# Score products on one half of the array's rows each, and experts selected by maximum and replacement

## What is computed

```python
def reference(x, w_q, b_q, w_k, b_k, w_v, b_v, w_o, b_o, gate_w, e_bias, up_w, down_w, shared_up_w, shared_down_w):
    h = layernorm(x)
    q, k, v = (heads(h @ w.T + b) for w, b in ((w_q, b_q), (w_k, b_k), (w_v, b_v)))
    attn = softmax(einsum('bhtd,bhsd->bhts', q, k) / sqrt(8))
    x = x + layernorm(einsum('bhts,bhsd->bhtd', attn, v) @ w_o.T + b_o)
    h = layernorm(x)
    scores = sigmoid(h @ gate_w.T)                      # [token, 32]
    sc = scores + e_bias
    group_scores = top_k(sc.reshape(T, 8, 4), 2)[0].sum(-1)
    kept = the 4 groups with the largest group_scores   # top_k: of equal ones the first
    idx = top_k(where(kept, sc, 0), 6)[1]
    w = scores[idx] / (scores[idx].sum(-1) + 1e-20) * 2.5
    f = sum over idx of w * relu(h @ up_w[e].T)**2 @ down_w[e].T + relu(h @ shared_up_w.T)**2 @ shared_down_w.T
    return x + layernorm(f)
```

## Time and profile before

| | |
|---|---|
| time, median of 3 runs | 581.74 us (580.57 to 582.0) |
| profiled execution: its own time | 586.01 us |
| span of that execution, first to last instruction | 584.0 us |
| PE busy | 539.0 us (92%) |
| PEld busy | 317.0 us (54%) |
| DVE busy | 422.9 us (72%) |
| ACT busy | 434.9 us (74%) |
| POOL busy | 148.2 us (25%) |
| mean granted TensorE clock | 0.962 |

### The profile page before, as it was taken

How to read it: one execution, slowest core, us unless ns; L and a number is a source line. 1 busy time by engine, 2 the same in 40 slices (tenths; PEclk the granted TensorE clock), 3 DMA queues, 4 the chain that set the end, 5 groups by cost and what they waited for, 6 DMA issues and landing times.

```text
span 584.0 us, 10389 instructions
## 1 busy us (share of the span) xinstructions
PE 539.0 (92%) x3248; PEld 317.0 (54%) x3248; DVE 422.9 (72%) x1116; ACT 434.9 (74%) x879; POOL 148.2 (25%) x439
## 2 busy tenths in 40 slices
PE   2478998999999999999989999999999999999993
PEld 1224554556655556555546665656566565656551
DVE  6676685788888778778857968686885868576343
ACT  2326676788888878776788787979888797977773
POOL 6141121213243223221102114224042423202010
PEclk9559798999999999999999999999999999999997
DMA  6333374233333333323000000000000000000001
GB/s 176 105 113 89 106 237 122 86 103 102 103 103 93 108 111 94 93 91 97 18 3 1 1 1 1 19 1 1 20 0 20 0 20 1 17 2 1 19 0 36
DMA packets 42774, 33.75 MB, mean 58 GB/s; under 512 B 4032, under 2 KB 35392, under 8 KB 42464
## 3 DMA queue, kind: packets, MB, share of 16 engines
q1 hardware_dynamic: 42720, 33.09, 18.6%
HBM read 18.01 MB, written 14.68 MB: 56 GB/s over the span
## 4 chain that ended last, share of the span: by engine, by line
PE 72%; DMA 8%; SPq 8%; ACT 5%; DVE 4%; issue 2%; POOL 0%; ACTq 0%; DVEq 0%
PE pY L1184 11%; PE pS L1184 11%; PE pO L1101 7%; PE pS L1089 6%; PE pS L1161 6%; PE pS L1163 6%; PE pS L1078 6%; PE pS L1162 6%; PE pS L1170 5%; DMA k_scratch<-k_parts 4%; DMA kp<-k_scratch 4%; SPq L369 3%; SPq L357 3%; ACT probs L557 3%; SPq L377 1%
## 5 line engine op out<-in xcount | busy, mean ns | idle before, releaser
L771 DVE TENSOR_REDUCE mneg<-pS 128x2 f32<-128x512 f32 x256 | 164.2, 686 | 37.6 <-PE pS L1078 36.2
L557 ACT ACTIVATE probs<-pS 128x512 f32<-128x512 f32 x256 | 140.9, 599 | 47.5 <-PE pS L1089 46.5
L947 DVE TENSOR_TENSOR h_ring<-pS,rr 128x512 f32<-128x512 f32 x128 | 88.3, 690 | 75.6 <-ACT rr L634 73.4
L625 ACT ACTIVATE r<-pS 128x512 f32<-128x512 f32 x144 | 85.7, 595 | 42.4 <-PE pS L1163 37.7
L1078 PE MATMUL pS<-kp,qp 96*128 96x256 bf16 x512 | 103.2, 287 | 12.3 <-DMA kp<-k_scratch 11.6
L1089 PE MATMUL pS<-qp,kp 102*128 102x512 bf16 x256 | 99.7, 392 | 4.5 <-ACT probs L557 2.8
L634 ACT ACTIVATE rr<-r 128x512 f32<-128x512 f32 x128 | 80.9, 632 | 4.0
L1161 PE MATMUL pS<-qp,up_hi 128*128 128x512 f32 x144 | 82.7, 574 | 0.1
L1078 PEld LDWEIGHTS pS<-kp,qp 96*128 96x128 bf16 x512 | 45.3, 101 | 58.7 <-DMA kp<-k_scratch 15.7
L1184 PE MATMUL pS<-h_ring,down_sb 128*128 128x512 f32 x144 | 73.5, 592 | 0.0
L1184 PE MATMUL pY<-h_ring,down_sb 128*128 128x512 f32 x144 | 73.0, 592 | 0.0
(11 more groups left out here) (182 smaller groups left out, 758.1 us busy)
## 6 DMA issues: line engine op xcount, KB each, us to landing
qp<-q_scratch SPq DMA_DIRECT2D x64, 96.0 KB
kp<-k_scratch SPq DMA_DIRECT2D x64, 96.0 KB
q_scratch<-q_parts SPq DMA_DIRECT2D x16, 192.0 KB, 2.0
k_scratch<-k_parts SPq DMA_DIRECT2D x16, 192.0 KB, 2.1
q_scratch<-q_parts SPq DMA_DIRECT2D x16, 128.0 KB, 1.9
k_scratch<-k_parts SPq DMA_DIRECT2D x16, 128.0 KB, 2.0
out_x<-ot SPq DMA_DIRECT2D x7, 256.0 KB, 2.3
q_scratch<-q_parts SPq DMA_DIRECT2D x16, 64.0 KB, 1.7
```

What stands on the lines that cost most here:

```text
L557: nc.scalar.activation(probs[j][:, sh], pS2[n % S2_RING][:, :, :], ACT.Exp, scale=SCALE).then_inc(exp_done, 1)
L625: nc.scalar.activation(r_sb[k % 2][:, :], pU[k % 2], ACT.Relu).then_inc(relu_done, 1)
L771: nc.vector.tensor_reduce(mneg[u % 2][:, :, hh, k], pS1[n % S1_RING][:, :].rearrange("p (a s) -> p a s", a=TH), AX.X, ALU.max, negate=True ...
L947: nc.vector.tensor_tensor(h_sb[n % HRING], pC[k % 2], r2_sb[k % 2][:, :], ALU.mult).then_inc(h_done, 1)
```

## The change

Scores: head `hh` = 0 now stands in rows 0 to 50 (48 and 3 for the maximum) and `hh` = 1 in rows 64 to 114. A product takes one head's rows alone, so 48 or 51 rows in one half of the array, and `qp` needs no zeros. The key product is now made per head, 2 x 128 keys by 256 queries, instead of for two heads at once. In `scores_by_both` the products alternate: queries' of one head, keys' of the other, and again, each time in the other half of the rows. Both waits (for `max_done` and `exp_done`, at a unit's first step also `packed` and `m_packed`) stand ahead of the four. `probs` is laid out by head first. The preset zeros of `qp` go away; the ones of `kp` now lie at two places of each slot. `x_cut`, `x_hi`, `x_lo` of the experts' part get other places.

Experts: MAX8 gives the largest 8, `match_replace` replaces the 4 (6) largest by a marker, first occurrence first, and a comparison with the marker gives the selection. 23 waits in 8 steps.

```diff
-DIFF_ROWS = 2 * QK_ROWS + 2 * M_ROWS
+DIFF_ROWS = QK_ROWS + M_ROWS
+HALF = P // 2
+KEY_HEADS = (1, 0)
-ROUTE_AT = ((3, 4, 5, 6, 7, 8, 9, 10, 11, 12, 13, 14),
-            (0, 1, 2, 3, 4, 5, 6, 8, 9, 11, 12, 13))
+ROUTE_AT = ((3, 4, 5, 6, 7, 8, 9, 11),
+            (0, 1, 2, 3, 4, 5, 6, 8))
...
-               ((5, 6), (7,), (), (8, 9), (10, 11), (), (), ()))
+               ((), (5,), (), (6,), (7,), (), (), ()))
...
-                    rows = slice(QK_ROWS * hh, QK_ROWS * (hh + 1))
-                    for dst, scratch in ((qp[u % RING][rows, hh], q_scratch), (kp[u % RING][rows], k_scratch)):
+                    rows = slice(HALF * hh, HALF * hh + QK_ROWS)
+                    for dst, scratch in ((qp[u % RING][rows], q_scratch), (kp[u % RING][rows], k_scratch)):
...
             write_parts(0)
-            sp.wait_ge(preset, 1)
             sp.wait_ge(ones_set, 1)
...
-            for i in range(RING):
-                ins = nc.gpsimd.memset(qp[i][:, :, :, :].rearrange("p a b c -> p (a b c)").bitcast(F32), 0.0)
-            ins.then_inc(preset, 1)
...
-                for sh in range(TH):
-                    n = TH * (NBLK * b + j) + sh
+                for i, hh in enumerate(KEY_HEADS):
+                    n = 2 * (NBLK * b + j) + i
                     act.wait_ge(s2_done, n + 1)
-                    nc.scalar.activation(probs[j][:, sh], pS2[n % S2_RING][:, :, :], ACT.Exp,
+                    nc.scalar.activation(probs[j][:, hh], pS2[n % S2_RING][:, :, :], ACT.Exp,
...
+            def take_best(link, values, n, best, at, left):
+                for c in range(C4):
+                    ins = nc.vector.max(top8[:, c], values[:, c, 0:n])
+                link(ins)
+                link(nc.vector.tensor_copy(best[:, :, 0:at], top8[:, :, 0:at]))
+                for c in range(C4):
+                    ins = nc.vector.match_replace(left[:, c], best[:, c], values[:, c], TAKEN)
+                link(ins)
...
             for i in range(RING - 1):
-                nc.vector.memset(kp[i][2 * QK_ROWS:P, :, :], 1.0)
+                for hh in range(2):
+                    nc.vector.memset(kp[i][HALF * hh + HALF // 2:HALF * (hh + 1), :, :], 1.0)
...
+            def query_scores(u, k, hh, th):
+                slot, n = u % RING, 2 * (UB * u + k) + hh
+                rows = slice(HALF * hh, HALF * hh + QK_ROWS)
+                return mm(pS1[n % S1_RING][:, T * th:T * (th + 1)], qp[slot][rows, k, P * th:P * (th + 1)],
+                          kp[slot][rows, k, :], start=True, stop=True)
+
+            def key_scores(u, k, i, sh):
+                slot, n = u % RING, 2 * (UB * u + k) + i
+                rows = slice(HALF * KEY_HEADS[i], HALF * KEY_HEADS[i] + DIFF_ROWS)
+                return mm(pS2[n % S2_RING][:, sh], kp[slot][rows, k, P * sh:P * (sh + 1)], qp[slot][rows, k, :],
+                          start=True, stop=True)
...
+            def scores_by_both(uq, uk, k, i):
+                query_scores_free(uq, k, i)
+                key_scores_free(uk, k, i)
+                query_scores(uq, k, i, 0)
+                key_scores(uk, k, i, 0)
+                query_scores(uq, k, i, 1).then_inc(s1_done, 1)
+                key_scores(uk, k, i, 1).then_inc(s2_done, 1)
```

143 lines of the change are left out of this document (60 added, 83 removed).

## The result

The changed kernel takes 587.29 us (median of 4 runs, 584.82 to 591.46) where the kernel before takes 581.79 (580.57 to 582.0): a ratio of 1.0104, with an interval from 1.0063 to 1.0144. Forecast were 572.4 us and a range of 562 to 584. So the change makes the kernel slower by some 5.5 us, and the forecast had the sign wrong. The profiled execution took 586.76 us, its span is 585.0.

The account below looks back on a forecast made before the run. PE was taken to bound the good attention batches and loads others; terms of 3.2 − 2.0 − 7.2 − 1.2 − 2.4 − 0.5 + 0.8 = −9.3 us took the span to 574.7, and from the median 572.4 us was forecast, range 562 to 584.

Parts of the forecast that it names:

- start, to the first exponential: Before the first scores: six DVE presets instead of three delay the whole chain, +3.2 us, bounds +2.5 and +3.2.
- batches 0 to 3: First attention batches, with slow loads or a low clock: hanging mostly in loads, they gain 0.5 us each, 2.0 in all.
- batches 7 to 9: Attention batches held by a loop of write, landing and load: only 0.4 us gained each, 1.2 in all.
- batches 13, 14: Late attention batches with almost no loads, where DVE also loses some selection work: 1.2 us gained each, 2.4 in all.
- batch 15: Last attention batch, with keys' products alone, two in the same half after one another: 0.5 us gained.
- clock: Waits before batches 8 to 10 grow, so the granted clock may fall there too: +0.8 us, bounds 0 and +4.
- Steps abreast: Score products in different row halves run abreast: a step takes 0.22 us instead of 0.44, 3.5 us less PE work per batch.
- The six good batches: Batches 4 to 6 and 10 to 12, bound by PE: from 15.95 us on average to about 14.7, 7.2 us gained.
- within the 0.4: First step's queries' product also waits for the maximum's rows, 177.10 instead of 176.83; covered by batches 7 to 9's 0.4 us each.
- the clock falls in most batches: Rival: PE waits at each batch's start and the clock falls to half; +12 us on the forecast, 584 us; chance 0.08.
- Changes of shape: PE switching array shapes in a middle batch: 20 changes instead of 12, 0.1 us each, 0.8 us more per batch.
- Selection: Expert selection on DVE, 38 waits to 23: saves some 3 us a tile, 0 for seven tiles; batches 13 to 15 counted separately.

Follow-up runs that it names:

- e4_route: The kernel before with only the new selection of experts; 582.63 us, ratio 0.9989.
- e12_half_exp: The changed kernel with loads cut to one DMA of four from unit 4 on and exponentials over half the queries from batch 1 on; 559.01 us, one run.
- e2_order: The changed kernel with each step's queries' products first behind their own wait, then the keys' products behind theirs; 586.13 us, ratio 1.0026.
- e6: The kernel before with each unit's q and k load cut to one DMA of four from unit 4 on; 573.23 us, ratio 0.9818.
- e5: The changed kernel with each unit's q and k load cut to one DMA of four from unit 4 on (e5_after_cut); 571.28 us, ratio 0.9785.
- e3_serial: The changed kernel with queries' products ahead of keys', each with its own wait, and all four products of a step in one row half; 591.3 us, ratio 1.016.
- e7_fill: The changed kernel with the first pair of products of every score step made twice; 590.17 us, ratio 1.0117.

## Why the prediction was wrong, step by step

The sum compared profile with profile and then subtracted 4.3 us, by which the profiled execution of the kernel before lay above its median. Both halves failed. The span was forecast to shrink by 9.3 us and grew by 1.0. And the profiled execution of the changed kernel lay 0.5 us below its median, so the 4.3 wasn't to be had again: it was time at half clock (10.2 us in that trace, 3.4 in e4_route's, whose attention is the same code and 4.1 us shorter), and not an offset that a changed kernel inherits. Of the miss of 14.9 us some 10 are the sum's and near 5 are this anchor's. (The bounds of the terms, as given, add up to 564 to 581, where the prediction wrote 566 to 580; nothing hangs on it.)

The terms, from the two traces:

| term | forecast | measured |
|---|---|---|
| start, to the first exponential | +3.2 | +2.7 |
| batches 0 to 3 | −2.0 | −2.5 |
| batches 4 to 6 and 10 to 12 | −7.2 | +1.5 |
| batches 7 to 9 | −1.2 | −0.75 |
| batches 13, 14 | −2.4 | −0.8 |
| batch 15 | −0.5 | +0.9 |
| clock | +0.8 | within the batches above |
| tiles | 0 | +0.1 |

*Steps abreast*: right, 0.22 us. By the Trainium skill's rule on weight loads ("TensorE: Matmul & The Clock Gate", LDWEIGHTS) the prediction estimated 0.43 us for four of them. It doesn't bind here: two loads into different halves start together, 0.09 us each.

*The six good batches* are the step that failed: forecast −7.2 us, measured +1.5. It had three errors. First, the floor: forecast 14.7, measured 15.27. The prediction set it by SP's queue and let the engines' turns cost 15.1 at most; the exponentials on ACT bound the batch (e12_half_exp), and it lasts 15.28 with no load in the way. Second, the joint wait ahead of the four products, judged "within the 0.4" at a unit's first step only: it acts at every step and costs 0.3 us of each batch (e2_order), some 1.8 of these six. With loads cut the six batches gain 2.6 us (95.7 in e6, 93.0 in e5), so these two errors together are 4.6 us of this term's miss. Third, 4.1 us: these batches weren't out of the loads' reach. The prediction counted loads as bounding seven batches and the queue as needing 14.1 us in the others, from a batch where the write landed in 1.2 us. With PE ready sooner the load waits lie in more places: batches 4 and 10, 15.8 us each before, are 16.9 and 16.6, each with 3.4 us at half clock behind a load wait of 0.67 and 1.36 us, and batches 6 and 12 end in waits of 0.80 and 0.83.

*The clock* was right in mechanism and wrong in size. The rival "the clock falls in most batches", at a chance of 0.08, gave 584 us and is the nearest to the result. Forecast for the main case was one more half of a fall; there were five falls, 20.4 us, against 10.2, and halves in the middle of attention were one of its own signs of being wrong. The prediction read 2.29 us as a wait that brings a fall and 1.05 as one that doesn't. No such length stands in the traces: ahead of three of the falls the load wait was 0.67 to 0.73 us, each with a second idleness behind it, for DVE or ACT, of 0.63 to 0.92 us; and 1.22 us in the middle of batch 2 brought none, nor did 1.46, 1.09 and 1.79 in e4_route. The price of 3.4 us at half clock was put at 0.7 to 1.0 us; by the batches beside e5_after_cut it is 1.3 to 1.5, and 8.0 us in all.

*Start*: the term was right to 0.5 us; DVE's delay was 3.7 us (4.07 to 7.73), more than forecast by the wider gap, and 1.0 of it was covered behind it. *Changes of shape*: their 0.8 us a batch was not told apart by a run. PE's busy time in batch 11 came to 13.8 us where 13.0 was forecast, but since PE's work didn't end the batch, little hung on it. *Selection*: 0 for the tiles was right; for batches 13 to 15 the forecast counted a gain and e4_route shows a shift, 0.4 us out of batch 14 and 0.8 into batch 15.

What is left open: why the landing of the same write takes 1.2 us in some batches and 3.3 in others, and why some load waits bring the clock down and longer ones don't.

## What to carry to other kernels

When an engine that was the bound gets faster, read what it will wait for from the chain of waits in the longest batches, not in the shortest, and count those as the rule: a faster engine meets a late transfer in more places. Here its waits for loads added up to the same as before, and what they set off in the clock cost more. Work taken off the matrix engine is worth only what the next partner's banks let through (here 0.5 of 1.9 us), and halving one engine's work in a run of its own says which partner that is, where the name beside a joint wait may be wrong. A run with loads cut, laid beside its kernel batch by batch, tells which batches a wait and which the clock makes longer. A wait put ahead of several instructions is paid by the one that didn't need it; and the distance of one profiled execution from the median isn't carried over to another kernel.

## What the runs showed of the hardware

Two matmuls in rows 0 to 47 and 64 to 114 of the array run fully abreast, 0.01 us apart, as do their weight loads (0.09 us each). A product may start ahead of one that stands before it in the program, if that one waits for its own half of the rows: in e2_order at 225.23 and 225.34, and in e3_serial across two steps. The granted clock, 1.00 (2.4 GHz) otherwise in batches 1 to 14, went to 0.50 (1.2 GHz) for 3.4 or 6.8 us at a time. Nearly always (30 of 33 falls) that was behind idleness of PE for a load, of 0.67 us or more, while waits of up to 1.79 us brought nothing; 3.4 us at half clock made a batch 1.3 to 1.5 us longer. A preset of 32 partitions x 1024 bf16 on DVE takes 0.91 us and a gap of 0.25; POOL sets four whole slots of 128 x 512 f32 in 1.91 us. The same six writes of parts, all from SP's queue, land 1.2 to 3.4 us after their last issue in most batches, and up to 4.9 us (e7_fill) in batch 2.
